# TensorE's order in the main loop of two attention layers: single units in place of pairs

## What is computed

```python
# layer 0: 16 heads of width 8, rotary positions, a bias that depends on the positions
scores = einsum('bhqd,bhkd->bhqk', q, k) * SCALE + temporal_bias(256, 1601)
attended = einsum('bhqk,bhkd->bhqd', softmax(scores), v) @ Wout.T + b_out
gate = sigmoid(attended @ Wgate.T + b_gate)
x = x + gate * attended + (1 - gate) * layernorm(x)
x = x + tanh(layernorm(x) @ w @ a1 @ a2 + bias)
# layer 1: the same shape without rotary positions and bias, then 8 experts, top 2
x = x + softmax(q k / sqrt(8)) v @ wo.T + bo
x = x + sum_of_top_2_experts(layernorm(x)) / 2
```

## Time and profile before

| | us |
|---|---|
| median of 3 runs | 614.51 |
| lowest and highest | 613.78, 618.03 |
| the profiled execution's own time | 611.3 |
| its span, first to last instruction | 609.3 |
| granted clock of TensorE, mean over the span | 0.969 |

### The profile page before, as it was taken

One profiled execution on the slowest core, in us unless ns is written; L12 is line 12 of the kernel. 1 busy time (PEld: TensorE's weight loads), 2 busy tenths in 40 slices (PEclk: granted clock), 3 DMA queues, 4 the chain that ended last, 5 costly groups with the idle time before them and its releaser, 6 DMA issues.

```text
span 609.3 us, 15184 instructions
## 1 busy us (share of the span) xinstructions
PE 545.9 (90%) x6325; PEld 268.4 (44%) x6325; DVE 280.4 (46%) x719; ACT 432.4 (71%) x492; POOL 183.3 (30%) x206
## 2 busy tenths in 40 slices
PE   6578899998999999999999999999999999999970
PEld 3354454444444554455554445444443444344330
DVE  5543845755585345653331243234353445344064
ACT  1226667665768677687778887898979888997901
POOL 6775837475668024760101000100000000000000
PEclk8869999999999999999999999999999999999976
DMA  8592484529656611462650066018412901000000
GB/s 193 126 269 84 134 278 134 173 75 303 159 160 193 218 28 31 146 211 95 143 149 28 28 156 152 29 30 193 114 38 79 212 18 38 29 2 5 5 2 12
DMA packets 42151, 68.13 MB, mean 112 GB/s; under 512 B 10855, under 2 KB 31983, under 8 KB 42078
## 3 DMA queue, kind: packets, MB, share of 16 engines
q1 hardware_dynamic: 33358, 41.03, 26.2%
q0 software_dynamic: 6416, 24.84, 12.5%
q10 hardware_dynamic: 2304, 1.25, 0.9%
HBM read 35.20 MB, written 18.83 MB: 89 GB/s over the span
## 4 chain that ended last, share of the span: by engine, by line
PE 64%; ACT 12%; DVE 8%; issue 7%; DMA 5%; POOL 2%; ACTq 0%; DVEq 0%; POOLq 0%
PE ps L444 24%; PE ps L428 12%; ACT probs L1013 10%; PE ps L422 8%; PE ps L368 4%; DMA mask_q<-in_mask 2%; PE ps L530 2%; PE ps L360 2%; DMA ctx_tokens<-in_ctx 2%; PE ps L362 1%; PE ps L456 1%; ACT k_parts L1040 1%; DMA q_side<-q_parts 1%; PE ps L480 1%; PE ps L493 1%
## 5 line engine op out<-in xcount | busy, mean ns | idle before, releaser
L1013 ACT ACTIVATE probs<-ps 124x1024 f32<-124x1024 f32 (+1 forms) x416 | 399.6, 1024 | 100.1 <-PE ps L428 98.0
L444 PE MATMUL ps<-probs,values 124*9 124x256 f32 (+1 forms) x3328 | 218.6, 380 | 2.4 <-DVE out_sums L1346 2.4
L428 PE MATMUL ps<-q_side,k_side 63*124 63x256 bf16 (+1 forms) x1664 | 161.9, 279 | 13.1 <-ACT probs L1013 11.3
L428 PEld LDWEIGHTS ps<-q_side,k_side 63*124 63x124 bf16 (+1 forms) x1664 | 96.1, 131 | 90.2 <-ACT probs L1013 62.1
L444 PEld LDWEIGHTS ps<-probs,values 124*9 124x9 f32 (+1 forms) x3328 | 70.7, 90 | 93.1 <-issue 37.4
L422 PE MATMUL ps<-bias_g,bias_w 64*124 64x512 bf16 (+1 forms) x416 | 85.3, 407 | 9.7 <-ACT probs L1013 8.0
L896 POOL TENSOR_TENSOR post_rstd<-post_rstd,power 128x2 f32<-128x2 f32 x12 | 8.4, 702 | 157.3 <-DVE post_rstd L1452 98.8
L422 PEld LDWEIGHTS ps<-bias_g,bias_w 64*124 64x124 bf16 (+1 forms) x416 | 27.4, 128 | 52.9 <-ACT probs L1013 30.8
L842 POOL DMA_DIRECT2D mask_q<-in_mask x16 | 9.0, 560 | 134.8 <-DVE checks L1322 113.9
L1263 DVE SCALAR_TENSOR_TENSOR k_swapped<-ps,beta_products,k_sin_sb 32x496 f32<-32x496 f32 (+2 forms) x64 | 40.4, 632 | 0.9
L1332 DVE TENSOR_REDUCE sample_max<-ps 128x8 f32<-128x512 f32 x32 | 20.5, 685 | 42.9 <-PE ps L388 42.9
(11 more groups left out here) (218 smaller groups left out, 535.3 us busy)
## 6 DMA issues: line engine op xcount, KB each, us to landing
k_side<-k_scratch SPq DMA_DIRECT2D x24, 400.2 KB, 9.0
k_side<-k_parts SPq DMA_DIRECT2D x48, 124.0 KB, 2.4
k_scratch<-k_parts POOLq DMA_DIRECT2D x16, 372.0 KB, 4.4
v_scratch<-values POOLq DMA_DIRECT2D x4, 936.0 KB, 9.2
values<-v_scratch SPq DMA_DIRECT2D x4, 936.0 KB, 14.6
v_scratch<-v POOLq DMA_DIRECT2D x12, 288.0 KB, 4.2
mask_q<-in_mask POOLq DMA_DIRECT2D x8, 400.5 KB, 3.8
mask_q<-in_mask POOLq DMA_DIRECT2D x8, 400.0 KB, 3.5
```

Source lines behind the costliest of these rows:

```text
L428: last = pe.matmul(ps[0:width, bank, SQ * i:SQ * (i + 1)], kst[rows, j % 2, 2 * g + i, at], qst[rows, j % 2, 2 * g + i, :], start=not bias ...
L444: last = pe.matmul(ps[32 * i:32 * i + VC, ACC + g // 2, SQ * (g % 2):SQ * (g % 2) + SQ], v[0:rows, j % 2, t, h, :], p[0:rows, u % 4, SQ * ...
L1013: act.activation(p[0:rows, u % 4, :], ps[0:rows, s:s + 2, :].rearrange("p a n -> p (a n)"), ACT.Exp)\
```

## The change

Only the body of the loop changes. TensorE takes one unit at a time: the scores of unit u + 2, then the side step of slot u of the stage, then the values of unit u. No instruction is added or removed: the 416 score steps stay in their order, so do the 416 value steps and the side steps. What changes is how these three lists are merged. A side step of an odd slot stood behind the values of its own unit and now stands ahead of them, behind the scores of u + 2. A side step of an even slot stood behind the scores of u + 3 and now stands ahead of them. ScalarE's, VectorE's, GpSimd's and SyncE's lists are the same.

```diff
@@ -639,15 +639,11 @@
 
                 pe.matmul(ps[:, ACC + n, :], zeros[:], zeros[:].unsqueeze(1).broadcast_to((128, 4, 128)),
                           start=True, stop=True, skip_group_check=True)
-            for u in range(0, NJ * UB, 2):
-                j, pair = u // UB, u % UB // 2
-                for w in (u + 2, u + 3):
-                    if w < NJ * UB:
-                        scores(w)
-                beside(j, 2 * pair)
-                for w in (u, u + 1):
-                    values(w)
-                beside(j, 2 * pair + 1)
+            for u in range(NJ * UB):
+                if u + 2 < NJ * UB:
+                    scores(u + 2)
+                beside(*divmod(u, UB))
+                values(u)
             pick(NJ - 1)
             for k in range(2):
                 experts(NB - 1, k)
```

## The result

The changed kernel takes 636.9 us in the median of four runs (632.5 to 643.3), the kernel before 615.9 beside it: a ratio of 1.033, 95% interval 1.028 to 1.038. It is slower, and by 21 us, not by the 14 forecast. 636.9 lies at the very top of the stated range. The ratio leaves out the slowest of the four, 643.3 us, which had the lowest mean clock (0.947).

What follows compares the result with a forecast made beforehand. TensorE was taken to bound the first half, with both engines near their limit in the second. Hand-overs +54, stalls -41 and pace +1 gave +14 on 614.5: 628 us, 2.3% slower, range 619 to 637.

Steps and rivals of the forecast that it cites:

- The hand-overs: TensorE's switches between scores and values: one more each way per pair, +0.26 us a pair, +54 us over 208 pairs.
- The rival by which the weight load hides the hand-over: At values-to-scores, weights load while values stream: 575 us with no hand-over price, 602 at half price; chance 0.04.
- The stalls: TensorE's waits for exponentials at a pair's second scores, plus 2.5 us at first units, all go: -41 us.
- ScalarE's pace: Second half, units without side step: TensorE waits up to 0.03 us a unit for ScalarE, 1 to 4 us.
- the +1: The amount in us taken into the sum for TensorE waiting on ScalarE's exponentials in the second half.
- the rival built on it (634 us): ScalarE paces the second half and side-step losses are never caught up: +6 us at 0.94 a unit, 634 us; chance 0.15.
- The 0.94 us: Distance between exponentials in a run of 12 on ScalarE, some waits for scores among them; set against TensorE's 0.91 a unit.
- Side steps: Odd-slot steps move between scores and values: step cost unchanged, each moves some 0.6 us, pair price stays +0.26.
- The nearest deadline: The shift for the next stage: last step in slot 39 or 40, needed in slot 50, ten units, over 9 us.
- its sum: First half of the loop: 104 pairs x 0.26 = 27 us of hand-overs less 13 of stalls, +14 us.
- its 3.4: Stalled second units without bias already pay 0.16 for their first score couple: 69 x 0.05 = 3.4 us, within the -41.
- The rival by which they shrink: Side steps' waits for partners, some 10 us, shrink as partners get more time; if 8 us go, 620 us; chance 0.11.

Runs made afterwards that it cites:

- lag2: The changed kernel with ScalarE's two gate activations of a batch two units behind their slot instead of three: 625.4 us, ratio 1.016.
- lag4: The changed kernel with ScalarE's two gate activations four units behind their slot instead of three: 666.1 us.
- pairs_lag2: The kernel before, in pairs, with ScalarE's two gate activations two units behind their slot: 615.4 us, ratio 1.001.
- pairs_then_units: Pairs as in the kernel before in stages 0 to 3, single units as in the changed kernel in stages 4 to 7: 618.9 us, ratio 1.006.

## Why the prediction was right or wrong

**The hand-overs: right.** +0.26 a pair shows in every plain pair, in both halves, and with ScalarE out of the way. The drain that the Trainium skill, "TensorEngine Tiling (Array Packing)", Key Properties, has at a change of tiling mode stands behind the new hand-overs of the plain pairs as far as distances can show it. Where a side step stands between, the distances sum to 1.3 us less in the first half than the forecast has. The rival by which the weight load hides the hand-over is refuted.

**The stalls: right.** TensorE's waits for exponentials at the scores are gone, ScalarE's waits for scores rose from 98.0 to 117.1 us, and the second half came out level: 226.9 with 2.7 of waits at L480 and 3.4 us at half clock, 222.9 with the shorter lag. ScalarE's pace cost nothing that can be seen; the +1 and the rival built on it (634 us) were wrong. The 0.94 us had waits in it, as the prediction says: in both kernels exponentials that follow each other directly start every 0.90 to 0.92 us, as in this run of eight of the changed kernel, (7.48 - 1.02) / 7 = 0.92:

```profile
489.31 7.48 ACT L1009 ACTIVATE probs<-ps 113x1024 f32<-113x1024 f32 x8
```

That is TensorE's own 0.91, not more. That 636.9 still lies within the range is luck: the room above 628 was there for this pace, and what filled it was another wait and the clock.

**Side steps: this step failed.** It said that each step moves by some 0.6 us, named the shift as the nearest deadline, and took the order of ScalarE's list as untouched and so as harmless. The list was untouched, but it is written in units behind a slot, and a slot's place among the scores moved. The nearest deadline was three units away, not ten. Price: 8.9 us (9.7 against 0.8), shown by taking the wait away (lag2) and by making it larger (lag4); with the clock that went with it, up to 11.8. It was to be had from the code: the lags of `gate` beside the place of each slot.

**The clock: not in the sum.** The forecast took the full clock as given. The granted share varies between executions of both kernels. At an equal mean clock of 0.970 the changed kernel took 632.5 and 632.9 us and the kernel before 611.8, 612.9, 613.0 and 614.6, so some 20 us are the order and its waits. The changed kernel's eight executions had 0.947 to 0.970 and 0.961 in the mean, and within them 632.5 us at 0.970 and 643.3 at 0.947 make 4.7 us per 0.01; a line through the 43 executions of the kernel before beside these runs has the same slope. They lay between 0.957 and 0.974, 0.966 in the mean. So the clock adds about 2 us to the median.

**The ledger.** Span 609.3 to 631.0, +21.7: the loop +20.3, its start and the tail +1.4. In the loop +8.9 at L480 and about +1.5 for 3.4 us at half clock leave +9.9 for what was forecast as +14. The second half's share is -0.7 (forecast 0), the first's +10.7 (forecast +14).

Three terms make up the 3 us by which the first half lost less than its sum. The hand-overs at side steps cost 1.3 less, as said. At 26 stalled second units TensorE already paid 0.265 us from bias to scores instead of 0.219, as a lone unit does; that is 1.2 us which the prediction counted without bias (its 3.4) and left out with bias. And the kernel before was not at full clock at the start of its loop: stage 0, first in its trace, then in that of pairs_lag2, which has the same order there and no fall of the clock, takes 1.1 us less in the second:

```profile
41.50:134.70 93.20, 86.43 (x871) 45.42 (x869) 55.82 (x152) 60.16 (x72) 58.76 (x54) 0.98 0.49 159
42.50:134.60 92.10, 85.08 (x871) 44.16 (x869) 55.70 (x152) 60.12 (x72) 58.98 (x54) 1.00 0.50 162
```

Other waits of side steps grew by some tenths of a us. The rival by which they shrink is not seen.

## What to carry to other kernels

When two engines' lists are tied by counts ("three units behind the slot"), a change of one list's order changes every such distance: list each wait of the moved steps with its partner's place, not only the farthest deadline. Interleaving two kinds of work on TensorE to fill a stall can pay only where the stall is longer than the added hand-overs, here 0.26 us a pair. Even at the longest stalls it gained only 0.5% here, since part of the stalls stayed or came up at the next places.

## What the runs showed of the hardware

I had not expected that waits of a few microseconds in a loop that is otherwise full would cost more than themselves. With eight waits of 2.0 to 2.5 us in the loop (lag4) seven stretches of 6.8 to 10.2 us at 1.2 GHz came with them, and cost over twice what the lengthening of the waits did (20 us against 8.5); with waits of 1.0 to 1.6 us the clock fell behind some of them in some executions; with none at these places (lag2) it did not fall there, though it did once behind two waits of 1.7 and 1.6 us early in stage 1. A wait on TensorE is then dearer by what follows it, and shows as such in the clock column, not in the waits.

Not every fall belongs to the order. Early in stage 1 the clock fell in seven of the eleven traces, in pairs_then_units too, where the order up to there is that of the kernel before:

```profile
146.10:152.90 6.80, 6.80 (x52) 3.22 (x50) 2.35 (x11) 1.94 (x2) 4.23 (x4) 0.50 1.05 362
```

In the kernel before it did not, with the same two waits there (1.4 and 1.6 us). Single traces can't tell what such a fall hangs on; that lag4 fell at seven of its eight waits, and that its four executions all had a lower mean clock (0.921 to 0.936) than any other run, is what ties the clock to the longer waits.
